# A quantized FFN kernel: x rows load ahead of unit 2, unit 0 quantized in halves, mixing and sums reordered at the start

## What is computed

```python
w = weights[subjects]                      # one 64x64 matrix for each sample
y = einsum('bct,bcd->bdt', x, w)           # "mixing"
gu = einsum('bsd,hd->bsh', y, ternary_quant(w_gate_up))
h = silu(gate) * up
x = x + einsum('bsh,dh->bsd', rms_norm(h), ternary_quant(w_proj))
# second layer: a linear with adapters, a router of 512*8 logits, top 2 of 8, experts
x = x + L1_ffn(L1_cond(x))
```

## Time and profile before

| what | us |
|---|---|
| median of 3 runs (lowest, highest) | 2292.76 (2292.17, 2292.88) |
| the profiled execution's own time | 2291.85 |
| its span | 2290.2 |
| TensorE busy | 2279.5 |
| VectorE busy | 1680.4 |
| ScalarE busy | 1149.2 |
| DMA, mean over the span | 83 GB/s |

### The profile page before, as it was taken

How to read it: one execution, slowest core, us unless ns; L and a number is a source line. 1 busy time by engine, 2 the same in 40 slices (tenths; PEclk the granted TensorE clock), 3 DMA queues, 4 the chain that set the end, 5 groups by cost and what they waited for, 6 DMA issues and landing times.

```text
span 2290.2 us, 30002 instructions
## 1 busy us (share of the span) xinstructions
PE 2279.5 (100%) x10212; PEld 1883.2 (82%) x10220; DVE 1680.4 (73%) x2522; ACT 1149.2 (50%) x1690; POOL 11.3 (0%) x20
## 2 busy tenths in 40 slices
PE   8999999999999999999999999999999999999999
PEld 6778888888888888888888888888888888888887
DVE  8976444343434346888899999998988888888883
ACT  8754323232323335888888888888322222222221
POOL 0000000000000000000000000000000000000000
PEclk9999999999999999999999999999999999999999
DMA  6304212213140317211111212115322222222220
GB/s 217 107 31 140 77 56 57 75 37 90 22 112 0 92 37 258 83 60 60 64 69 55 78 59 74 60 60 225 120 83 95 68 93 82 78 96 81 80 83 23
DMA packets 154026, 191.04 MB, mean 83 GB/s; under 512 B 62898, under 2 KB 96242, under 8 KB 151666
## 3 DMA queue, kind: packets, MB, share of 16 engines
q1 hardware_dynamic: 110690, 135.26, 18.2%
q10 hardware_dynamic: 43152, 55.06, 7.3%
q0 software_dynamic: 128, 0.07, 0.0%
HBM read 129.01 MB, written 61.34 MB: 83 GB/s over the span
## 4 chain that ended last, share of the span: by engine, by line
PE 98%; DVE 1%; ACT 1%; DMA 0%; issue 0%; ACTq 0%; SPq 0%; DVEq 0%
PE slot L1686 20%; PE pj L1701 10%; PE plane L1842 10%; PE plane L1844 10%; PE plane L1846 10%; PE ex L1882 10%; PE ex L1883 10%; PE ex L1884 10%; PE slot L1753 4%; PE slot L1630 1%; PE slot L1742 1%; DVE ew_lo L1540 1%; PE slot L1640 0%; PE slot L1759 0%; PE slot L1758 0%; PE slot L1757 0%
## 5 line engine op out<-in xcount | busy, mean ns | idle before, releaser
L1686 PE MATMUL slot<-y_hi,wgu 128*128 128x512 f32 x1016 | 398.2, 392 | 0.4 <-DVE y_lo L1157 0.4
L1686 PE MATMUL slot<-y_lo,wgu 128*128 128x512 f32 x1016 | 395.6, 389 | 0.0
L1842 PE MATMUL plane<-rw_hi,hb 128*128 128x512 f32 x1008 | 392.3, 389 | 0.0
L1844 PE MATMUL plane<-rw_hi,hb 128*128 128x512 f32 x1008 | 392.1, 389 | 0.0
L1846 PE MATMUL plane<-rw_lo,hb 128*128 128x512 f32 x1008 | 392.1, 389 | 0.0
L1882 PE MATMUL ex<-ew_hi,hb 128*128 128x512 f32 x992 | 386.0, 389 | 0.2 <-ACT ex L1095 0.2
L1884 PE MATMUL ex<-ew_lo,hb 128*128 128x512 f32 x992 | 385.9, 389 | 0.0
L1883 PE MATMUL ex<-ew_hi,hb 128*128 128x512 f32 x992 | 385.9, 389 | 0.0
L1095 ACT ACTIVATE ex<-eb_sb 128x512 f32<-128x512 f32 x248 | 148.9, 602 | 449.8 <-DVE acc L1569 386.8
L1515 DVE SCALAR_TENSOR_TENSOR lead_in<-code_in,wts 128x1024 bf16<-128x1024 bf16 x256 | 311.9, 1218 | 1.2
L1686 PEld LDWEIGHTS slot<-y_hi,wgu 128*128 128x128 f32 x1016 | 190.7, 188 | 43.1 <-DVE q_scale L1164 1.9
(11 more groups left out here) (179 smaller groups left out, 3226.9 us busy)
## 6 DMA issues: line engine op xcount, KB each, us to landing
hb<-h_scratch SPq DMA_DIRECT2D x34, 512.0 KB, 3.3
code_scratch<-half_code SPq DMA_DIRECT2D x64, 256.0 KB, 2.0
half_in<-code_scratch SPq DMA_DIRECT2D x32, 512.0 KB, 3.3
hb<-h_scratch ACTq DMA_DIRECT2D x30, 512.0 KB, 3.6
h_scratch<-ht ACTq DMA_DIRECT2D x48, 256.0 KB, 3.0
q_raw<-in_w_ffn SPq DMA_DIRECT2D x21, 512.0 KB, 3.4
x_scratch<-x_res ACTq DMA_DIRECT2D x8, 1024.0 KB, 4.4
rraw<-in_rwT SPq DMA_DIRECT2D x8, 1024.0 KB, 8.7
```

The lines of the kernel that those rows point to most:

```text
L1686: last = mm(slot[s % 2][:, g, :], wgu[:, c, r * P:(r + 1) * P], y[:, c, :], start=(c == 0 and v == 0), stop=(c == DC - 1 and v == 1))
L1842: mm(bank[:, :, :], hb[:, u, c, 0, :], rw_hi[:, w, c, o], start=False, stop=False, skip_group_check=True)
L1844: mm(bank[:, :, :], hb[:, u, c, 1, :], rw_hi[:, w, c, o], start=False, stop=False, skip_group_check=True)
```

## The change

- ScalarE issues unit 0's rows in two DMAs of 512 columns, then, behind the load of its function table, unit 1's, and when the first half of unit 0 is in, the rows `x_mix` of block 0; unit 2's come last. `first_in` makes Abs of each half, and `first_quant` on TensorE and VectorE makes sums and floor of each half by itself.
- On VectorE the memset of `ones_col` comes first, and SyncE and GpSimd wait for one more memset.
- TensorE does `mix(0)` ahead of unit 2's sums, and those of units 3 and 4 behind gu(0,0) and gu(0,1), unit 5's behind gu(0,2). Unit 3's sums go to the projection's PSUM pair too (`EARLY`), so `q3` leaves the list `FIRST`; `q5` moves behind `gu2@0`. The dummies ahead of `mix(0)` become 4 + 2 in place of 4 + 3 + 5, those behind it 6 in place of 8.
- ScalarE does `mix(0)` ahead of `quant_mean(2)`, and changes its order up to the first pass of the loop (h = 1). VectorE does unit 3 and unit 4 whole instead of in two parts with other work between, and in the first pass `product(0, 2)` ahead of unit 5.

```diff
@@ -71,9 +71,9 @@
 AHEAD = 2
 GU_ORDER = []
-FIRST = ["q0", "q1", "mix0@0", "mix1@0", "q3"]
+FIRST = ["q0", "q1", "mix0@0", "mix1@0"]
 PAIRS = HC // 2
-EARLY = [2, 4]
+EARLY = [2, 3, 4]
 MEANS = [1, 2, 3, 4, 5] + [3 * _h + 4 for _h in range(1, PAIRS - 1)]
@@ -86,6 +86,8 @@
     _j = 2 * _h
     FIRST.append(f"gu{_j}@0")
     GU_ORDER.append((0, _j))
+    if _h == 1:
+        FIRST.append("q5")
     if _h:
         FIRST.append(f"gu{_j - 2}@1")
         GU_ORDER.append((1, _j - 2))
@@ -96,7 +98,7 @@
         FIRST.append(f"gu{_j - 1}@1")
         GU_ORDER.append((1, _j - 1))
     else:
-        FIRST += ["mix0@1", "mix1@1", "q5"]
+        FIRST += ["mix0@1", "mix1@1"]
     FIRST += [f"q{k}" for k in quant_of(_h)[2:]]
 SECOND = ["ss"] + [f"gu{_j}" for _j in range(HC - AHEAD, HC)] + ["t0", "t1", "xa", "h0", "h1"]
 GU_ORDER += [(1, _j) for _j in range(HC - AHEAD, HC)]
@@ -462,7 +468,7 @@
                 sp.dma_start(hid1[:, second_slot(p), :], hid_dram[r]).then_inc(hid1_in[second_slot(p)], 16)
             sp.dma_start(subject_i[:, :], idx7).then_inc(subject_in, 16)
-            sp.wait_ge(dconst, 2)
+            sp.wait_ge(dconst, 3)
             sp.wait_ge(subject_in, 16)
             gather_mix(0, mixw, mixw_in, range(SPB // 2))
@@ -660,7 +666,7 @@
         @block.gpsimd
         def _(pool):
-            pool.wait_ge(dconst, 1)
+            pool.wait_ge(dconst, 2)
             pool.wait_ge(subject_in, 16)
             for q in range(SPB // 2, SPB):
                 v = pool.value_load(subject_i[0:1, q:q + 1], min_val=0, max_val=E - 1)
@@ -716,10 +722,21 @@
                 nc.scalar.activation(q_mag[:, k % 3, :], q_raw[:, k % 3, :], ACT.Abs).then_inc(q_in, 1)
                 nc.scalar.activation(q_sign[:, k % 3, :], q_raw[:, k % 3, :], ACT.Sign).then_inc(q_in, 1)
+            def first_in():
+                act.dma_start(q_raw[:, 1, :], w_ffn[1]).then_inc(qraw_in[1], 16)
+                act.wait_ge(first_raw, 16)
+                nc.scalar.activation(q_mag[:, 0, 0:D], q_raw[:, 0, 0:D], ACT.Abs).then_inc(first_mag, 1)
+                act.dma_start(x_mix[:, :, :], one(XB, 0)).then_inc(xmix_in, 16)
+                act.wait_ge(qraw_in[0], 16)
+                nc.scalar.activation(q_mag[:, 0, D:UW], q_raw[:, 0, D:UW], ACT.Abs).then_inc(q_in, 1)
+                nc.scalar.activation(q_sign[:, 0, :], q_raw[:, 0, :], ACT.Sign).then_inc(q_in, 1)
+                act.dma_start(q_raw[:, 2, :], w_ffn[2]).then_inc(qraw_in[2], 16)
             def quant_mean(k):
                 if k in EARLY:
-                    sums = pj_pair[EARLY.index(k)]
+                    sums = pj_pair[k // 4]
                     act.wait_ge(early_filled, EARLY.index(k) + 1)
                 else:
                     n, s = use(0, f"q{k}")
@@ -850,47 +867,52 @@
                 act.wait_ge(x1_ready, (i + 1) * SUB)
                 act.dma_start(one(X1B, i), x_res[:, :, :]).then_inc(x1_stored, 16)
-            act.dma_start(q_raw[:, 0, :], w_ffn[0]).then_inc(qraw_in[0], 16)
-            act.dma_start(q_raw[:, 1, :], w_ffn[1]).then_inc(qraw_in[1], 16)
-            act.dma_start(q_raw[:, 2, :], w_ffn[2]).then_inc(qraw_in[2], 16)
-            act.dma_start(x_mix[:, :, :], one(XB, 0)).then_inc(xmix_in, 16)
-            act.wait_ge(dconst, 3)
+            act.dma_start(q_raw[:, 0, 0:D], w_ffn[0][:, 0:D]).then_inc(first_raw, 16)
+            act.dma_start(q_raw[:, 0, D:UW], w_ffn[0][:, D:UW]).then_inc(qraw_in[0], 16)
+            act.wait_ge(dconst, 1)
             nc.scalar.activation(sq[:, 0:1], ones_col[:, :], ACT.Silu).then_inc(table_in, 1)
-            quant_in(0)
+            first_in()
             quant_in(1)
+            quant_mean(1)
             quant_in(2)
-            quant_mean(1)
             quant_out(0)
+            mix(0)
             quant_mean(2)
-            mix(0)
+            quant_out(1)
             quant_in(3)
-            quant_out(1)
+            silu(0, 0)
             quant_mean(3)
             quant_in(4)
-            silu(0, 0)
             quant_out(2)
-            quant_mean(4)
             act.wait_ge(drained, use(0, "gu0")[0] + 1)
             square(0, 0, hid[:, 0, :])
             silu(0, 1)
             high(0, 0, hid[:, 0, :])
-            quant_in(5)
+            quant_mean(4)
             mix(1)
             quant_out(3)
+            quant_in(5)
             act.wait_ge(drained, use(0, "gu1")[0] + 1)
             high(0, 1, hid[:, 1, :])
-            quant_mean(5)
-            quant_in(6)
             square(0, 1, hid[:, 1, :])
             for h in range(1, PAIRS):
                 j = 2 * h
                 more = h < PAIRS - 1
-                if more:
-                    quant_in(3 * h + 4)
-                silu(0, j)
-                quant_out(3 * h + 1)
-                silu(1, j - 2)
-                quant_out(3 * h + 2)
+                if h == 1:
+                    silu(0, j)
+                    quant_mean(5)
+                    quant_out(4)
+                    quant_in(6)
+                    silu(1, j - 2)
+                    quant_in(7)
+                    quant_out(5)
+                else:
+                    if more:
+                        quant_in(3 * h + 4)
+                    silu(0, j)
+                    quant_out(3 * h + 1)
+                    silu(1, j - 2)
+                    quant_out(3 * h + 2)
                 act.wait_ge(drained, use(0, f"gu{j}")[0] + 1)
                 square(0, j, hid[:, j % 2, :])
                 if more:
@@ -1119,9 +1141,9 @@
         @block.vector
         def _(dve):
+            nc.vector.memset(ones_col[:, :], 1.0).then_inc(dconst, 1)
             nc.vector.memset(mixw[:, :, :], 0.0).then_inc(dconst, 1)
             nc.vector.memset(mixw1[:, :, :], 0.0).then_inc(dconst, 1)
-            nc.vector.memset(ones_col[:, :], 1.0).then_inc(dconst, 1)
             nc.vector.memset(group_mean[:, :], 0.0).then_inc(dconst, 1)
             dve.wait_ge(dconst, 4)
             for g in range(P // GROUP):
@@ -1163,6 +1185,17 @@
                 dve.wait_ge(filled, n + 1)
                 nc.vector.tensor_scalar(q_scale[:, :], slot[s % 2][:, :, :].rearrange("p a n -> p (a n)"),
                                         SCALE_FLOOR, None, ALU.max).then_inc(drained, 1)
+            def first_quant():
+                n, s = use(0, "q0")
+                dve.wait_ge(first_sum, 1)
+                nc.vector.tensor_scalar(q_scale[:, 0:D], slot[s % 2][:, 0, :], SCALE_FLOOR, None, ALU.max).then_inc(first_scale, 1)
+                dve.wait_ge(filled, n + 1)
+                nc.vector.tensor_scalar(q_scale[:, D:UW], slot[s % 2][:, 1, :], SCALE_FLOOR, None, ALU.max).then_inc(drained, 1)
+                dve.wait_ge(first_scale, 1)
+                quant_gap(0)
+                quant_sign(0)
             def quant_floor(k):
@@ -1313,28 +1346,28 @@
                 nc.vector.tensor_tensor(ht[:, :, 1, :], slot[s % 2][:, :, :], ht[:, :, 0, :].bitcast(F32),
                                         ALU.subtract).then_inc(drained, 1)
-            quant(0)
+            first_quant()
             quant(1)
             mix(0)
             quant(2)
-            quant_floor(3)
-            quant_gap(3)
             product(0, 0)
-            quant_sign(3)
-            quant_floor(4)
+            quant(3)
             product(0, 1)
-            quant_gap(4)
             low(0, 0, hid[:, 0, :])
             squares(0, 0)
             mix(1)
-            quant_sign(4)
+            quant(4)
             low(0, 1, hid[:, 1, :])
             for h in range(1, PAIRS):
                 j = 2 * h
                 more = h < PAIRS - 1
                 a, b = 3 * h + 3, 3 * h + 4
-                quant(3 * h + 2)
-                product(0, j)
+                if h == 1:
+                    product(0, j)
+                    quant(3 * h + 2)
+                else:
+                    quant(3 * h + 2)
+                    product(0, j)
                 squares(0, j - 1)
                 second_product(j - 2)
                 if more:
@@ -1640,11 +1673,21 @@
                     last = mm(slot[s % 2][:, b, :], group_mean[:, :], q_mag[:, k % 3, b * D:(b + 1) * D], start=True, stop=True)
                 last.then_inc(filled, 1)
+            def first_quant():
+                n, s = use(0, "q0")
+                pe.wait_ge(first_mag, 1)
+                mm(slot[s % 2][:, 0, :], group_mean[:, :], q_mag[:, 0, 0:D], start=True, stop=True).then_inc(first_sum, 1)
+                pe.wait_ge(q_in, 1)
+                mm(slot[s % 2][:, 1, :], group_mean[:, :], q_mag[:, 0, D:UW], start=True, stop=True).then_inc(filled, 1)
             def early_sums(k):
                 pe.wait_ge(q_in, 2 * k + 1)
+                if k == 3:
+                    pe.wait_ge(mean_ready, MEANS.index(2) + 1)
                 for b in range(2):
-                    last = mm(pj_pair[EARLY.index(k)][:, b, :], group_mean[:, :], q_mag[:, k % 3, b * D:(b + 1) * D],
```

(23 more changed lines are left out.)

## The result

| | us |
|---|---|
| kernel after, median of 20 runs (lowest, highest) | 2295.83 (2293.94, 2297.41) |
| kernel before, the 20 runs beside them | 2291.98 (2291.21, 2292.88) |
| ratio, 95% interval | 1.0017 [1.0011, 1.0023] |
| the profiled execution of after, its span | 2297.0, 2295.3 |

The change costs 3.8 us. Its runs also spread over 3.5 us, those of before over 1.7. The forecast was 2292.4, and the time lies above the range (2290.9 to 2294.7). Against the kernel before it was a gain of 0.4 us.

The account below looks back on a forecast made before the run. TensorE bounds the kernel, so the start of gu(0,3) sets the end. Starting unit 2's floor on VectorE earlier gains 0.86 us, the new orders lose 0.43: 0.4 us earlier, 2292.4 us, range 2290.9 to 2294.7.

Parts of the forecast that it names:

- What bounds: TensorE behind 70 us: goes from matmul to matmul, so a shift of gu(0,3)'s start passes to the end one for one.
- B: Rival at the head: loads interleave better, gathers and unit 2 land by 10.5 us; 1.1 us earlier, 2291.4; chance 0.20.
- Unit 0 in halves: VectorE's start: unit 0 done at 9.7 us instead of 11.25, 1.55 us earlier, bounds 0 to 2.1.
- The loads: Head DMAs: x_mix lands near 9.4 us, unit 2 at 11.2, last gather at 11.0, at the latest 12.1.
- The clock: TensorE at mix(0): fast clock has risen by then and holds, nothing lost; mix(0) takes 3.81 us.
- Rival C: TensorE pauses from 8.8 us, half of mix(0) runs at 1.2 GHz; 1.1 us later, 2293.8; chance 0.20.
- C's full case: All of mix(0) slow from 12.1 us and gu(0,0) slow too: 5.9 us later, 2298.6; chance 0.04.
- the main sum: The forecast itself, over the whole kernel: 0.4 us earlier, 2292.4, by itself 2292.0 to 2292.9; chance 0.47.
- The orders: Moved sums of units 3, 4, 5: gu(1,0) waits for product(0,2), and gu(0,3) loses 0.43 us.
- F: Moment VectorE begins unit 2's floor: forecast at 17.4 us instead of 18.26, a gain of 0.86 us.
- mixing ahead: mix(0) ahead of unit 2's sums: starts at 11.0 us, ends at 14.8; VectorE begins unit 2's floor at 17.3 to 17.4.
- The sign that I gave for being wrong: At the head, VectorE's start of unit 2's floor moving by over 1.5 us would show the forecast wrong.

Follow-up runs that it names:

- the second execution: Profiled execution of the kernel after run again with no edit; median 2295.59 us, ratio 1.0018 to the kernel before.
- fewer dummies: Kernel before without the 3 and the 5 dummies ahead of unit 2's sums and of mix(0); 2293.96 us, ratio 1.0008.
- mix(0) ahead: Kernel before with mix(0) ahead of unit 2's sums on TensorE and of quant_mean(2) on ScalarE, same dummy work; 2292.75 us, ratio 1.0003.
- units 3 to 5: Kernel before up to mix(0), with the kernel after's orders and slot list from there on; 2292.75 us, ratio 1.0002.
- the pair with 14 dummies: Kernel after with 14 dummies instead of 2 ahead of mix(0), 2293.53 us; the same with units 1, 2 and x_mix issued up front, 2293.08 us.
- loads of before: Kernel after with units 1, 2 and x_mix issued up front behind unit 0's halves, 2 dummies; 2295.22 us, ratio 1.0013.
- dummies kept: Kernel after with 14 dummy sums instead of 2 ahead of mix(0); 2293.53 us, ratio 1.0007.
- orders of before: Kernel after with 14 dummies, and the kernel before's orders and slot list from unit 3's sums on; 2293.64 us, ratio 1.0007.
- x_mix ahead in before: Kernel before with x_mix issued ahead of unit 2, both up front; 2296.25 us, ratio 1.0018.

## Why the prediction was wrong

**What bounds, and that it passes one for one: right.** Span less the start of gu(0,3) is 2247.0 us before and 2246.8 after; in the other twelve executions 2246.7 to 2247.3. The head was the right place to look, and one number was enough. (The base was 0.8 us high: 2292.76 from 3 runs, where 20 runs give 2291.98. The forecast gain of 0.4 us stands against a measured loss of 3.8. B's 2291.4 doesn't follow from its 1.1 us either; that gives 2291.7. Neither changes the answer.)

**Unit 0 in halves: right in time, worth nothing.** First q_scale at 4.89 us (4.75 forecast), unit 1's floor at 9.95 (9.7). In the kernel before it moved the time by no more than the interval. The DMA issue inside the table load was right too (1.83 us, 0.5 later than before, where the least delay was put at 0.7).

**The loads: wrong, the first step that failed.** I let x_mix and unit 2 trade places: x_mix at 9.4 us, unit 2 at 11.2. They landed at 12.1 and 13.6, and at 10.6 and 12.4 in the second execution. And I set the landing of the last gather, 12.1 us, as the latest possible; it came at 14.0, 13.0, 13.2 and 13.7 us in four executions with the new loads, against 12.1 (before), 12.6 (fewer dummies), 12.6 (mix(0) ahead), 11.9 (units 3 to 5) and 12.9 (in the kernel after) with those of before. One profiled execution gave one draw, and I took it for a bound. Nor did that execution show TensorE waiting for a gather: its last dummies ended at 12.23 us, just when mix(0) began. What the loads cost in time is about 0.45 us, from the pair with 14 dummies, and their part in the pause.

**The clock: the term that failed most. It was named, but the sum put it at nothing.** The forecast took mix(0) at 3.81 us, on the ground that the clock "has risen by then and holds". Neither half is so. In after the last dummies were still slow (1.06 us for two, in the second execution too); the prediction's own rows gave no ground for it: there the rise came 5.5 us behind the first sum, and its dummies were to end 4.6 us behind theirs (4.2 to 8.8 us). And in the two kernels with a pause of 3.1 us where the clock had risen (loads of before, fewer dummies) it did not hold.

Rival C has the mechanism: dummies done at 8.8 (9.5 in the profile), a pause until mix(0), 1.2 GHz. In C half of mix(0) was slow (1.9 us) from 11.0 us; it was 1.6 to 2.6 us more from 13.0 to 14.1. C's full case had mix(0) from 12.1 and slow throughout; gu(0,0), which it also slowed, ran at full speed (16 matmuls in 3.66 us). C decides where mix(0) ends behind 15.6 us; it ended at 20.5 and 18.5. I argued against it that the sums start 1.3 us earlier and the rise comes earlier. It doesn't follow: with the dummies kept the first sum was at 4.4 us and the weight loads close up only at about 11.0 us, as in before (10.9), and in the run with the orders of before from unit 3 on at about 8.7. The pause was in my own timeline, 8.8 to 11 us, and the rows held no price for it: I put 0.24 on C where the main sum itself produced its condition. Dummies up to the landing cure both faults, a clock that has not risen and one that falls; no run here parts the two within the kernel after. Filling the pause is worth 2.3 us in the kernel after, 2.1 in it with the loads of before, and 1.85 in the kernel before.

The Trainium skill (TensorE: Matmul & The Clock Gate, HAM oscillation) says that waits of TensorE between bursts of matmuls make it throttle again, so that the next burst starts slow. The kernel with fewer dummies and the kernel after with the loads of before agree: the sums ahead of the pause were fast, the clock read 0.50 behind a pause of 3.1 us in both, and 1.00 behind pauses of 1.2 and 1.9 us in others (mix(0) ahead; orders of before).

**The orders: right in kind, 0.43 us for 0.76.** gu(1,0) does wait 1.1 us for product(0,2). gu(1,0) is at F + 19.22 (I had 18.97) and needs 6.51 us to gu(0,3) (I had 6.43); VectorE's floor of unit 3 starts 0.75 us behind product(0,0) and not 0.60. But that mixing ahead costs as much under the orders of before, through unit 3's Abs, I had not seen; under the new orders it is hidden.

**Together.** Of after's 3.8 us, the slow clock behind the pause is 2.3, the loads 0.45, and 1.0 is left with both undone, of which the profile puts 0.8 on the orders. (The three add up to 3.8 by the way they are taken: they are the steps from after to before, and each is good to some 0.5 us.) The halves alone measured 0.4, an interval that includes zero, and nothing in the profile. The clock is settled by three pairs of kernels with their profiles, the orders by the profiles alone; the loads' 0.45 us is within the scatter of its pair. The sign that I gave for being wrong (F moving by over 1.5 us) came, with 4.5 and 2.5; the other, no idle time ahead of gu(1,0), did not. Why the last gather landed later with the new loads is open, and so is the spread of a microsecond between landings of the same kernel.

## What to carry to other kernels

If TensorE waits for a transfer at the head of a kernel, keep it in work until the latest landing that occurs, not the one of a single profile: the price of too few dummy matmuls is the slow clock under the first real work. Ahead of reordering loads, look which of them ends the wait; moving the large one ahead gains nothing where small gathers behind it are last. And count what stands between the freed step and the next shared resource: gu(0,0) nearly 1 us early was used up by a wait in front of gu(1,0).

## What was unexpected of the hardware

- The last gather, of 16 KB, took 4.6 to 6.9 us from issue to landing while the DMA engines were full (1.03 of their share at 335 GB/s from 10 to 12 us in after), and issuing it 0.7 us earlier on another queue did not make it land earlier (12.4 us against 11.9 to 12.6).
- x_mix, with 0.5 MB fewer ahead of it in its queue, landed at 10.6 to 12.1 us in five executions (after twice, dummies kept, orders of before, x_mix ahead in before), against 11.1 to 12.3 in four with the order of before (before, fewer dummies, mix(0) ahead, units 3 to 5). Unit 2 behind it landed at 12.4 to 13.6 instead of about 8. Order in the queue moved the loser by 4 to 5.5 us, and the winner by less than its own spread.
- The granted clock reads 1.00 ahead of the first matmuls, while they run 0.43 us apart, and 0.50 only after a pause: at the head the spacing of the weight loads tells the clock, the column does not. When that spacing halves varied too, from about 8.7 to 11.0 us, between kernels that all began their sums at 4.3 to 5.5.
